# Masking in the attention steps of a fused attention and FFN kernel: from a second matmul on the scores to the contraction, GpSimd and VectorE

## What is computed

```python
xn   = layernorm(x)                                   # no scale, no shift
mask = causal & (i - j < 128 | landmark[j])           # i query, j key
q, k, v = xn@Wq, xn@Wk, xn@Wv                         # 16 query heads, 8 kv heads, 16 wide
probs = softmax(q k^T / 4 + where(mask, 0, -10000))
s = (probs v) @ Wo
h = gelu(xn @ tern(w1).T + b1); g = silu(h @ tern(w2).T + b2)   # 1024 hidden
out = x + s * g
# landmark: norm and direction give each token a score; the best 337 of 1024,
# widened by two tokens on either side, are landmarks
```

## Time and profile before

| | us |
|---|---|
| median of three runs | 735.6 |
| the profiled execution, its own time | 737.96 |
| its span, first to last instruction | 736.3 |
| PE busy | 628.7 (85%) |
| ACT busy | 475.7 (65%) |
| DVE busy | 375.4 (51%) |
| POOL busy | 74.7 (10%) |
| mean granted TensorE clock | 0.935 |

### The profile page before, as it was taken

The page is one execution under the profiler, slowest core; times in us unless marked ns, Lnnn a source line. Parts: engine busy times, 40 slices in busy tenths (PEclk is TensorE's granted clock), DMA queues, the critical chain, the costliest instruction groups (busy, mean ns, idle before and its releaser), DMA issues. The chain is left out here.

```text
span 736.3 us, 11753 instructions
## 1 busy us (share of the span) xinstructions
PE 628.7 (85%) x4336; PEld 351.7 (48%) x4336; DVE 375.4 (51%) x1002; ACT 475.7 (65%) x723; POOL 74.7 (10%) x92
## 2 busy tenths in 40 slices
PE   0537809999999989999999679999999899799982
PEld 0524604664455546654554536654554556334532
DVE  7968961665827434767454615648364521410101
ACT  1112417677877766697768556697768666888680
POOL 4000020020010201020100301110100210201001
PEclk9968957999999979999999869999999899899997
DMA  7000699000145659001190756001082691030101
GB/s 214 0 0 1 83 89 153 9 8 20 47 62 77 73 116 144 16 8 31 35 124 21 83 143 102 11 8 58 16 115 37 80 137 42 7 90 8 52 10 49
DMA packets 46833, 43.84 MB, mean 60 GB/s; under 512 B 6065, under 2 KB 41394, under 8 KB 46770
## 3 DMA queue, kind: packets, MB, share of 16 engines
q1 hardware_dynamic: 44642, 41.18, 33.6%
q10 hardware_dynamic: 2128, 1.84, 0.8%
HBM read 11.28 MB, written 4.19 MB: 21 GB/s over the span
## 5 line engine op out<-in xcount | busy, mean ns | idle before, releaser
L812 ACT ACTIVATE probs<-sc_ps,shift 128x512 f32<-128x512 f32 (+1 forms) x288 | 175.8, 617 | 102.0 <-PE sc_ps L725 101.3
L718 PE MATMUL sc_ps<-q_stack,k_stack 99*128 99x512 bf16 (+3 forms) x768 | 198.5, 344 | 33.3 <-PEq L189 14.7
L815 ACT ACTIVATE probs<-sc_ps,key_bias 128x1024 f32<-128x1024 f32 (+3 forms) x256 | 204.9, 818 | 16.5 <-PE sc_ps L718 15.8
L738 PE MATMUL att_ps<-probs,v_sb 128*32 128x512 f32 (+3 forms) x1536 | 167.4, 508 | 0.0
L718 PEld LDWEIGHTS sc_ps<-q_stack,k_stack 99*128 99x128 bf16 x768 | 50.2, 99 | 182.9 <-issue 70.8
L725 PE MATMUL sc_ps<-near_mask,mask_ident 128*128 128x256 bf16 (+1 forms) x576 | 105.1, 266 | 0.0
L850 POOL TENSOR_TENSOR h_lo<-hid,h_hi 128x512 fp32r<-128x512 f32 x32 | 43.2, 1350 | 342.3 <-DVE h_hi L882 342.3
L725 PEld LDWEIGHTS sc_ps<-near_mask,mask_ident 128*128 128x128 bf16 x576 | 56.4, 103 | 37.5 <-issue 7.1
L665 PE MATMUL aux_ps<-w2T,h_hi 128*128 128x256 f32 x256 | 70.1, 307 | 0.0
L665 PE MATMUL aux_ps<-w2T,h_lo 128*128 128x256 f32 x256 | 63.2, 279 | 0.0
L773 ACT ACTIVATE hid<-aux_ps,b_sb 128x512 f32<-128x512 f32 x64 | 42.9, 687 | 22.8 <-PE aux_ps L655 13.8
(11 more groups left out here) (152 smaller groups left out, 748.9 us busy)
## 6 DMA issues: line engine op xcount, KB each, us to landing
q_stack<-q_parts SPq DMA_DIRECT2D x96, 128.0 KB, 8.1
k_stack<-k_parts SPq DMA_DIRECT2D x24, 256.0 KB, 8.8
xn<-in_L_attn_hidden_states SPq DMA_DIRECT2D x4, 1024.0 KB, 8.2
attT<-att_raw SPq DMA_DIRECT2D x128, 32.0 KB
rden_bc<-den SPq DMA_DIRECT2D x64, 64.0 KB
probs<-in_L_ffn_w SPq DMA_DIRECT2D x2, 1024.0 KB, 7.8
out_y<-xn SPq DMA_DIRECT2D x4, 512.0 KB, 6.1
xn<-in_L_attn_hidden_states SPq DMA_DIRECT2D x3, 512.0 KB, 4.0
```

The source lines that it names most:

```text
L718: last = pe.matmul(sc_ps[:, 2 * u + hh, lo:CH], k_stack[0:KROWS + SHIFT_ROWS, h // REP, kb * P:(kb + 1) * P], q_stack[0:KROWS + SHIFT_ROWS ...
L738: last = pe.matmul(att_ps[32 * q:32 * q + 32, n % 2, lo:CH], v_sb[:, kb, j * VW:j * VW + 32], probs[:, i % 3, q, lo:CH], start=(kb == 0), ...
L812: last = act.activation(probs[:, i % 3, us, lo:near], sc_ps[:, us, lo:near], ACT.Exp, bias=shift[:, 0:1], scale=HD ** -0.5)
L815: last = act.activation(probs[:, i % 3, us, near:CH], sc_ps[:, us, near:CH], ACT.Exp, bias=key_bias[:, kb:kb + 1], scale=HD ** -0.5)
```

## The change

The masking matmuls (L725) go, and three things take their place.

1. **Far keys.** The contraction grows from 99 to 104 rows. Eight rows of k_stack hold, for each key block, -1 where a key is no landmark, and eight rows of q_stack (later_tile) hold 32768 for the key blocks that lie far behind a query block. Their product is added to the score in the same matmul. The exp of a half is then one instruction over all its columns, with one bias.
2. **Diagonal block.** After both exps of a step, POOL clears the triangle of four heads in probs with one affine_select of 128x4x128 (causal, L1588).
3. **Block beside it.** DVE multiplies the same size in probs by a 0/1 block of bf16 (local, L1619).

values waits for both and moves to three steps behind; probs gets a fourth buffer. q is stacked by group into three slots instead of 16 heads (fill_q: 6 DMAs of 64 KB and one of 32 KB), k by group too (fill_k: 6 of 64 KB), and the far rows in one DMA (fill_far). Layer norm of the next batch starts at step 3 and not 5, and its inverse root and that of the token scores are cut into pieces over steps. The set-up and the two ways through the kernel (with and without exact row maxima) get their own tiles: one branch after the set-up in place of one in each turn, and a short block of memsets behind that branch. The way without row maxima runs here, before and after.

```diff
-    LAG = 2
+    NPROB, BEHIND = 4, 3
+    FREED_BY = {3: 0, 4: 1, 5: 2, 6: 3, 7: 4, NG: 6, NG + 1: 7, NG + 2: 5}
 def scores(i, u):
-    last = pe.matmul(..., k_stack[0:KROWS + SHIFT_ROWS, ...], q_stack[0:KROWS + SHIFT_ROWS, h, ...])
-    if near > lo:
-        last = pe.matmul(sc_ps[:, 2 * u + hh, lo:near], mask_ident[:, :], near_mask[:, first:end:kb + 1, :], ...)
+    last = pe.matmul(..., k_stack[0:KROWS + T, ...], q_stack[0:KROWS + T, SLOT[n], 2 * u + hh, lo:CH])
 def values(i):
     pe.wait_ge(exp_done, 2 * (i + 1))
+    if has_tri(i): pe.wait_ge(tri_done, TRIS[i])
+    if has_local(i): pe.wait_ge(local_done, LOCALS[i])
 def exps(i):
-    if near > lo: last = act.activation(probs[..., lo:near], sc_ps[..., lo:near], ACT.Exp, bias=shift[:, 0:1], ...)
-    if near < CH: last = act.activation(probs[..., near:CH], sc_ps[..., near:CH], ACT.Exp, bias=key_bias[:, kb:kb + 1], ...)
+    act.activation(probs[:, i % NPROB, us, lo:CH], sc_ps[:, us, lo:CH], ACT.Exp, bias=shift[:, 0:1], ...)
+def causal(i):                        # POOL
+    pool.wait_ge(exp_done, 2 * (i + 1))
+    pool.affine_select(out=block_probs, in_=block_probs, compare_op=ALU.is_ge, fill=0.0, ...)
+def local(i):                         # DVE, called at step i + 1
+    dve.wait_ge(exp_done, 2 * (i + 1))
+    dve.tensor_tensor(block_probs, block_probs, near[:, kb, :].unsqueeze(1).to_broadcast([P, NQ, P]), ALU.mult)
+def fill_q(n):                        # SP; n counts groups, n >= NG is the next batch
+    sp.wait_ge(sc_done, 2 * (GROUP_END[FREED_BY[n]] + 1))
+    ... 6 DMAs q_stack[:, SLOT[n % NG]] <- q_parts, 1 DMA <- later_tile
 def job q_proj:                       # ACT
-    act.wait_ge(stack_in[1], 16 * NPART * QT)
+    for slot in range(3): act.wait_ge(q_in[slot], 16 * (NPART + 1) * SLOT[3:GROUPS * (a[1] + 1)].count(slot))
 set-up, DVE:
-    dve.memset(q_stack[KROWS:KROWS + 32, :, :].bitcast(F32), 0.0)
-    lk(dve.memset(k_stack[KROWS:KROWS + 32, :, :], 1.0))
+block behind the branch, POOL: memsets of v_sb, lm_pad, count, den, later_tile; one affine_select of later_tile (8x1024)
```

More of the change, by code:

```diff
@@ L71, in sb, with named @@
             return ctx.enter_context(nc.sbuf_tensor(name, shape, dt))
[L73 to L78, removed]
+        def named(names, group):
+            for n in names.split():
+                group.append(ctx.enter_context(nc.semaphore(n)))
+            return group[-len(names.split()):]
         ident = sb("ident", [P, P])
@@ L99, in kernel_program @@
         xn = sb("xn", [P, T, D])
[L100 to L122, removed]
         stats = sb("stats", [P, T, 6])
@@ L186, in link @@
             return f
-        def clear_semaphores():
-            with nc.Block(no_gpsimd_drain=True) as block:
-                @block.sync
-                def _(sp):
-                    lo = min(s.num for s in sems)
-                    assert [s.num for s in sems] == list(range(lo, lo + len(sems)))
-                    sp.sem_clear(range(lo, lo + len(sems)))
         def rsqrt(dve, lk, m):
@@ L435, in _ @@
                     @block.tensor
                     def _(pe):
-                        for h in range(H):
-                            if h >= 2:
-                                pe.wait_ge(masked_done, h - 1)
-                            for half in range(NC):
-                                last = pe.matmul(sc_ps[:, 2 * (h % 2) + half, :], q_stack[:, h, bass.ds(t * P, P)],
-                                                 k_stack[:, h // REP, half * CH:(half + 1) * CH], start=True, stop=True)
-                            last.then_inc(sc_done, 1)
@@ L455, in _ @@
-                        for h in range(H):
-                            dve.wait_ge(sc_done, h + 1)
-                            ps = sc_ps[:, 2 * (h % 2):2 * (h % 2) + 2, :].rearrange("p a n -> p (a n)")
-                            dve.tensor_tensor(masked, ps, mask, ALU.add).then_inc(masked_done, 1)
-                            dve.wait_ge(masked_done, h + 1)
-                            lk(dve.tensor_reduce(row_max[:, h:h + 1], masked, AX_X, ALU.max))
-                        dve.tensor_scalar(row_max, row_max, -1.0, None, ALU.mult).then_inc(max_done, 1)
@@ L462, in _ @@
-                        lk(dve.tensor_scalar(query_at, query_at, float(P), None, ALU.add))
-                        dve.wait_ge(aux_first, 1)
-                        lk(dve.tensor_tensor(left, aux_ps[0:H, 0, 0:P], parts[:, 0, :], ALU.subtract))
-                        lk(dve.tensor_copy(parts[:, 1, :], left))
-                        dve.tensor_tensor(parts[:, 2, :], left, parts[:, 1, :], ALU.subtract).then_inc(max_split, 1)
+                        dve.wait_ge(pads_done, 1)
+                    @block.tensor
```

2243 lines of the change are left out of this document (1494 added, 749 removed).

## The result

The changed kernel takes **706.4 us** (median of 4 runs, 702.2 to 714.6) against 735.6: a ratio of 0.958, 95% interval 0.951 to 0.965. The forecast was 693, with 674 to 712 as its range. Of the 42 us forecast, 29 came. The slowest of the four counts as slow and the ratio leaves it out; the median of the other three is 703.0. The profiled execution took 702.98 with a span of 701.3, so what follows explains 35 us of difference against the profiled 737.96.

What follows compares the result with a forecast made beforehand. PE was taken as the bound, busy 19.6 to 20.0 of every 20 us. Terms -52.8 + 4 + 4.5 + 4.5 - 1.8 = -41.6 off 735.6 gave 694, stated as 693; range 684 to 702, with neighbouring rivals 674 to 712.

Steps and rivals of the forecast that it cites:

- masks off PE, with what ACT takes back: Attention steps: dropping the masking matmuls saves PE 52.8 us; steps without a job, where ACT binds, return 4 (0 to 10).
- multiplies on DVE: Attention steps: 112 multiplies at 0.69 to 1.67 us; late ones hold values, +4.5 us (0 to 24) over three preparing turns.
- triangles on POOL: Attention steps: 128 selects at about 0.9 us each, hidden because values need them over one step later; no cost.
- q copies behind the stack's transfer: q projection at step 26: ACT's copy waits for the stacking DMA, +4.5 us (0 to 25) over three turns.
- set-up and the new block: Before the first turn: two DVE memsets gone, -7 us (0 to -8.3); new memset block and barrier, +6.2 (4 to 9).
- turn ends: End of each turn: four branches become one and masks are no longer built there, -1 us (0 to -3).
- its own signs: Wrong if PE waits for DVE over 2 us a turn, a select passes 1.9 us, or job stages keep their masks' time.
- 1 us a turn, in the steps without a job: Attention steps without a job: ACT's exps limit the mask saving, +4 us in all (0 to 10).
- the term of 1.5 us a preparing turn for backlog: Three preparing turns: late DVE multiplies hold values, then ACT, then scores; +4.5 us in all (0 to 24).
- the two steps of distance: Attention steps: the two steps between a multiply and its values give back some 4 us of DVE backlog each time.
- DVE with POOL becomes the bound: Rival: in chunks 0 and 1 all multiplies wait for a triangle, 8 us a turn instead of 1.5; 712 us, chance 0.20.
- the quick landing: q stacking before step 26: transfer lands 1.5 us after issue rather than 8.1, so ACT's copy waits 1.7 us.

## Why the prediction was right in its sign and 13 us too low

By its own steps, forecast and measured:

| step | forecast | measured |
|---|---|---|
| masks off PE, with what ACT takes back | -52.8 + 4 | -39.0 |
| multiplies on DVE | +4.5 | +13.6 |
| triangles on POOL | 0 | +5 to +7 |
| q copies behind the stack's transfer | +4.5 | 5.0 of wait (1.3, 2.3, 1.4) |
| set-up and the new block | -0.8 | -3.7 |
| turn ends | -1 | -2.2 |

These rows add up to some -20, and 29 came. The runs that leave work out close the sum: masks away -39.0, then all the rest of the change without its clearing -9.7 (697.0 to 687.3), then the clearing +19.1. Of the 9.7, set-up and turn ends are 5.9, so the remainder, with the 5 us of q waits inside it, holds some 9 us of gain that the forecast had at 1: exps in one piece, values a step later, stacking by group. No run separates these. That 706 came out inside the range is in part luck: without that gain it would have been some 714.

By its own signs the forecast was wrong in two places. PE waits for DVE's multiplies 3.0 to 3.1 us in each preparing turn, over the 2 that it allowed, and the stages with jobs in chunk 1 of a preparing turn didn't shorten by their masks.

**Masks.** The mechanism was right: from scores to values PE now takes 0.54 us at full width (489.66 to 490.20) also where masks stood. Wrong was how much of it ACT lets through. I charged ACT with 1 us a turn, in the steps without a job; 52.8 against 44.4 in the attention steps is 8.4 us, twice the charge, and PE's waits for exps grew by 7.9 us when only the masks went. Of the further 5.4, the smaller stages took 3.4, and the rest lies between the medians and the profiled runs.

**The multiplies: the term that was most too small.** I priced them at 0.69 to 1.67 us each and that was right (0.77). What I mis-sized is the term of 1.5 us a preparing turn for backlog, against the 4 to 5 that leaving them out gave. I compared DVE's sum with PE's over 20 us windows and gave the two steps of distance back each time. But in the stretch from 488.7 to 501 DVE has no gap at all, so the second multiply inherits the lateness of the first, and the distance is given only once. The rival "DVE with POOL becomes the bound" named this at 8 us a turn; 4 to 5 is found for the multiplies and some 5 with the triangles. It priced a full collision for each, which hardly occurs (0.77 and not 1.67 in the mean), and so came nearer by a wrong mechanism.

**The q copies.** Place, releaser and size as forecast (488.01, 1.42 us; forecast 1.7 at the quick landing). Wrong was that PE "has a job meanwhile", so that it would cost no more than itself: moving it by a step gave 8.7 us (6.6 by stages). DVE's split waits with it just ahead of the dense stretch (1.23 us at 488.70), which fits, but no run takes the wait away and leaves that work in its place.

**The triangles** are hidden as instructions, as forecast, and not free: leaving them out gives 5 to 7 us, which I had at nothing.

**Set-up.** Thresholds at 16.61, just ahead of the 17 to 19 forecast; they come 8.7 us earlier, where 7 was forecast. The new block costs 4.7 us more than the barrier did before (6.3 from the end of shift to the first DVE row against 1.65), where 6.2 was forecast.

**Values three steps behind.** The forecast used the distance and set no price on it. After the masks it is the largest term here: 27 to 28 us. The third step was not tried in the kernel before, so how much of this covers the clearing, and how much would have helped without it, stays open.

**The statistics at step 3** were in the change, and no step of mine spoke of them.

Set-up and turn ends came out some 4 us better than forecast; the larger errors in priced terms ran the other way, toward 712.

## What to carry to other kernels

Work moved to an engine with a free share fits only if it fits in the stretch where that engine is dense; look there for its last gap, and from it on add up how late each instruction comes. Then try the place of that engine's deferrable work before anything else: two numbers in a job table gave 12 to 14 us here, where the whole rewrite had given 29. And when clearing, masking or scaling is moved behind the producer, give its consumer one more buffer of distance: without it the rewrite was worth 0.3%.

## What the runs showed of the hardware

Behind a wait of 2.4 us of PE in the middle of a full stretch the granted clock was 0.66 over the next 5 us, and four matmuls took twice their time (2.02 against 1.03 us). The same set-up and preparation got a granted clock of 1.00 or of 0.50 from 80 to 90 us in the executions of different variants, and came to its first exp at 105.5 or at 111 us. The changed kernel's runs go with the mean clock: 702.2 at 0.921, 703.0 at 0.920, 709.8 at 0.912, 714.6 at 0.906. The kernel before spread over 1.2 us beside them, and over 4 to 5 in two of the later measurements.

A triangle of 512 columns on POOL takes 0.63 to 0.66 us by itself and 1.15 when it starts 0.04 us behind a multiply of DVE on SBUF operands, while that multiply keeps its 0.69. Where POOL was first, DVE took longer: 0.65 and 0.55 us in place of 0.17, at 494.31 and 494.99. Both agree with the exclusion that the Trainium skill describes (SBUF — State Buffer, § Who interferes with whom), by which the one that issues first keeps the shared ports for its whole instruction. The 0.63 lies below the 769 ns that the Trainium skill gives as its best case over 512 elements (GPSIMD Engine Reference, § Elementwise — side-by-side cycle accounting); the measurement decides.
